# Second routed experts: inner units on the partitions, weights and biases loaded per block, no transposes between the products

## The chip, the cores and the metric

One core of one Trainium2 chip. The metric is the device time in microseconds (us) of one execution of the whole kernel, which is two transformer layers in one program. Five engines work side by side and meet at semaphores: TensorE (PE; its weight loads are listed as PEld), VectorE (DVE), ScalarE (ACT), GpSimd (POOL) and SyncE (SP, which here only issues DMAs).

## What is computed

`x` has 16 sequences of 256 rows of 128 numbers (4096 rows). Each layer is attention, layer norm, a mixture of experts, layer norm. The change is in the routed experts of the second layer:

```python
gates = xf @ router_w + router_b                      # 8 experts
topv, topi = jax.lax.top_k(gates, 2)
comb = einsum('nke,nk->ne', one_hot(topi, 8), softmax(topv))
h = gelu(einsum('nd,edh->enh', xf, w1) + b1[:, None, :])   # d = 128, h = 256
y = einsum('enh,ehd->end', h, w2) + b2[:, None, :]
moe_out = einsum('ne,end->nd', comb, y)
```

Two shared experts, which see every row, have the same form with weights `sw1`, `sw2` of their own. All data is float32.

## The kernel before

The program runs five stages one after the other, each with its own instruction stream per engine: `attention0`, `routed0` (first layer), `attention1`, `routed1` (second layer), `final1`.

`attention1` also routes: it scatters each normalised row twice, once for each of its two experts, into a table `xs` in memory, grouped by expert, with two more numbers behind the 128 of the row (where its result goes, and its first choice). In its last stretch, after the last sequence's attention, it computes the shared experts (`up`, `down`, `expert_hidden`, `expert_low`, 32 steps, L1589 on, L1768 on, L2202 on), the routing of the last two sequences, and on DVE a table of blocks (`table_counts` to `table_rows`): for each block of 256 rows its expert, the column of the expert's weights (`w_at`) and its first row in `xs` (`in_at`). Among these steps stand two pieces of set-up for `routed1`: the biases of the routed experts are fetched as rows on partitions 0 and 32 (SP, four small DMAs into `work`), `bias_high` rounds them and `bias_low` takes the rest (DVE, at steps 10, 11, 15 and 16), after a memset on POOL (L1932). Early in the stage SP loads the weights of all eight experts, 256 KB each, into `g.w` (L1268), where they stay.

`routed1` (L946 to L1090) goes over N = 39 blocks of 256 rows. For a block j:

- SP reads `in_at` into a register and loads the block's rows into one of 6 slots of `xrow` (L978 to L981); it waits for `dest_done`, that is for `destinations` of block j - 6.
- PE turns the rows (`turn_input`, two transposes, L1034), ACT copies the result to `x` (`turned`, L1057), two slots.
- `gate` (L1006, L1007): rows on the partitions, `x` is the stationary operand, the expert's 256 columns of `w1` stream by; a second product of ones with the bias rows adds the bias. ACT applies Gelu to 128x512 at once (L1052).
- `turn_hidden` (L1015): four transposes; DVE copies 128x512 from PSUM (`hidden_columns`, L1070).
- `down` (L1025, L1027): four products and two bias products; DVE copies 128x256 from PSUM to one of 4 slots of `yrow` (`output`, L1075).
- POOL scatters the 256 result rows to `yt` with two indirect DMAs (L989) to the rows in `dest`, which DVE computes (`destinations`, L1081).

The order on each engine is written out by hand. PE at step j: `gate(j)`, `turn_hidden(j - 1)`, `down(j - 2)`, `turn_input(j + 2)`. DVE at step j: `destinations(j)`, `hidden_columns(j - 1)`, `output(j - 2)`. `destinations(j)` overwrites the slot of block j - 4, so it first waits on `y_out`, which counts the landed scatters of block j - 4:

```python
dve.wait_ge(x_in[j % XSLOTS], (j // XSLOTS + 1) * 16)
after(dve, y_out[j % YSLOTS], j // YSLOTS * 32)
dve.wait_ge(xt_ps, j + 1)
```

DVE works in order, so `hidden_columns(j - 1)` and `output(j - 2)` stand behind this wait. `down(j)` waits for `y_done` of block j - 2 (two PSUM slots).

Of the kernel before, what the change touches and what calls it, by code (L numbers as in the profile page):

```python
# [12 lines left out]
F32 = mybir.dt.float32  # L13
# [8 lines left out]
P = 128  # L22
# [20 lines left out]
W1C = F1 + FB1 * P  # L43
LOW = 32
# [901 lines left out]
def routed1(nc, ctx, g, d):  # L946
# [3 lines left out]
    rc = lambda name: g.rc[:, RC[name][0]:sum(RC[name])]  # L950
    XSLOTS, YSLOTS = 6, 4
# [3 lines left out]
    xrow = sb("xrow", [P, XSLOTS, 2, XW])  # L955
    dest = sb("dest", [P, YSLOTS, 2], U32)
    x = sb("x", [P, 2, BR])
    hid, hid_t = sb("hid", [P, 2, 2, F1]), sb("hid_t", [P, 2, FB1, BR])
    yrow = sb("yrow", [P, YSLOTS, 2, P])
    G, HT, Y, XT = g.psum[:, 0:2, :], g.psum[:, 2:4, :], g.psum[:, 4:6, 0:BR], g.psum[:, 6:8, 0:BR]  # L960

    xt_ps, x_done, gate_ps, act_done, ht_ps, ht_done, down_ps, y_done, dest_done = (sem(n) for n in (
        "xt_ps", "x_done", "gate_ps", "act_done", "ht_ps", "ht_done", "down_ps", "y_done", "dest_done"))
    x_in = [sem(f"x_in{k}") for k in range(XSLOTS)]
    y_out = [sem(f"y_out{k}") for k in range(YSLOTS)]
# [7 lines left out]
    with nc.Block() as block:  # L973
        @block.sync
        def _(sp):
            for j in range(N):
                after(sp, dest_done, j - XSLOTS + 1)
                at = nc.values_load(in_at[0:1, j:j + 1], engines=(mybir.EngineType.SP,), min_val=0, max_val=XROWS - BR,  # L978
                                    skip_runtime_bounds_check_because="the table's rows are clamped")
                sp.dma_start(xrow[:, j % XSLOTS], g.xs[bass.ds(at, BR)].rearrange("(h p) f -> p h f", p=P)  # L980
                             ).then_inc(x_in[j % XSLOTS], 16)  # L981

# [12 lines left out]
        def _(pe):  # L995
            w = {}
            bias = g.q_stk[:, 0].rearrange("p h t -> p (h t)")

            def gate(j):
                w[j] = nc.values_load(w_at[0:1, j:j + 1], engines=(mybir.EngineType.PE,), min_val=0, max_val=(E1 - 1) * W1C,  # L1000
                                      skip_runtime_bounds_check_because="the table's rows are clamped")
                pe.wait_ge(x_done, j + 1)
                after(pe, act_done, j - 1)
                for h in range(2):
                    out = G[:, j % 2, h * F1:(h + 1) * F1]
                    nc.tensor.matmul(out, x[:, j % 2, h * P:(h + 1) * P], g.w[:, bass.ds(w[j], F1)], start=True, stop=False)  # L1006
                    last = nc.tensor.matmul(out, g.ones[:], bias[:, bass.ds(w[j] + P, F1)], start=False, stop=True)  # L1007
                last.then_inc(gate_ps, 1)

            def turn_hidden(j):  # L1010
                pe.wait_ge(act_done, j + 1)
                after(pe, ht_done, j - 1)
                for f in range(FB1):
                    for h in range(2):
                        last = nc.tensor.transpose(HT[:, j % 2, f * BR + h * P:f * BR + (h + 1) * P], hid[:, j % 2, h, f * P:(f + 1) * P],  # L1015
                                                   g.ident[:])
                last.then_inc(ht_ps, 1)

            def down(j):
                pe.wait_ge(ht_done, j + 1)  # L1020
                after(pe, y_done, j - 1)
                for h in range(2):
                    out = Y[:, j % 2, h * P:(h + 1) * P]
                    for f in range(FB1):
                        nc.tensor.matmul(out, hid_t[:, j % 2, f, h * P:(h + 1) * P], g.w[:, bass.ds(w[j] + (F1 + f * P), P)],  # L1025
                                         start=f == 0, stop=False)
# [1505 lines left out]
```

## Time and profile before

| | |
|---|---|
| median of 3 runs | 1634.45 us (1633.99 to 1639.09) |
| the profiled execution: its own time | 1633.04 us |
| its span in the profile | 1631.2 us |
| PE busy | 1392.3 us (85%) |
| DVE busy | 1077.9 us (66%) |
| ACT busy | 895.7 us (55%) |
| POOL busy | 647.9 us (40%) |
| `routed1`, first load issued to last scatter issued | 1436.8 to 1577.3 us |
| shared experts | 1378 to 1435 us |

Busy time counts an engine's instructions; matmuls are pipelined and their ends are modelled, so the time of one matmul in a row (its latency) is longer than the distance between two starts, and a PE busy for 90% of a stretch is not at 90% of its peak. Idle time is put down to what came last before the engine went on; "issue" there means that the profile shows nothing that it waited for, and records of DMA landings are incomplete in this trace.

### The profile page before, as it was taken

The page shows a single profiled execution, that of the slowest core. Times are in us where ns is not written, and L with a number is a line of the kernel's source. Part 1 is how long each engine was busy: PE and PEld are TensorE (multiplying, and loading weights), DVE is VectorE, ACT ScalarE, POOL GpSimd, SP SyncE. Part 2 cuts the span into 40 slices and gives each one's busy share as a digit, 9 for nine tenths or more (in the row PEclk, how much of TensorE's full clock was granted, in tenths as well). Part 3 has the DMA queues.
Part 4 walks back from the last instruction along what each step waited for, and adds up shares of the span by engine and source line. Part 5 has one row for each costly group of instructions (what it writes and reads, how often), then busy time and mean ns, then how long its engine had stood idle before and what let it go on. Part 6 is the DMA issues. An engine that isn't in the chain of part 4 may idle for free. (4 is left out here: it accounts for less than half of the span.)

```text
span 1631.2 us, 35670 instructions
## 1 busy us (share of the span) xinstructions
PE 1392.3 (85%) x10839; PEld 1132.1 (69%) x10840; DVE 1077.9 (66%) x3450; ACT 895.7 (55%) x2391; POOL 647.9 (40%) x978
## 2 busy tenths in 40 slices
PE   5999999999999998299998269999999998988840
PEld 4777777777777777188887157777777776778740
DVE  4777777777777776266665358888888874833326
ACT  3656666666666665055554136777666766832213
POOL 1344444444444444133333232344445333325542
PEclk9999999999999999599999559999999999999975
DMA  6112020202020200011111621022214000023214
GB/s 219 52 36 72 20 73 19 73 19 73 19 73 19 74 22 13 21 42 47 48 46 38 215 67 53 30 73 73 74 47 150 7 15 15 14 67 83 79 59 126
DMA packets 59992, 96.36 MB, mean 59 GB/s; under 512 B 11140, under 2 KB 49412, under 8 KB 57432
## 3 DMA queue, kind: packets, MB, share of 16 engines
q1 hardware_dynamic: 50632, 76.47, 15.3%
q0 software_dynamic: 8864, 18.43, 3.3%
q8 instruction: 34, 0.56, 0.1%
q10 hardware_dynamic: 432, 0.66, 0.1%
q14 instruction: 30, 0.25, 0.1%
HBM read 75.01 MB, written 61.60 MB: 84 GB/s over the span
## 5 line engine op out<-in xcount | busy, mean ns | idle before, releaser
L362 POOL TENSOR_TENSOR a_prob<-a_prob,a_rl 128x128 f32<-128x128 f32 (+1 forms) x258 | 125.5, 508 | 256.1 <-DVE a_rl L447 255.8
L250 ACT ACTIVATE a_prob<-psum,a_nmx 128x128 f32<-128x128 f32 (+1 forms) x516 | 212.3, 423 | 11.9 <-DVE a_nmx L442 11.9
L1989 DVE TENSOR_REDUCE a_mx<-psum 128x2 f32<-128x512 f32 x256 | 170.8, 689 | 41.8 <-PE psum L1320 38.1
L276 ACT ACTIVATE a_probt<-psum 128x768 f32<-128x768 f32 x128 | 103.9, 811 | 118.9 <-PE psum L639 118.9
L1680 ACT ACTIVATE a_prob<-psum 128x1024 f32<-128x1024 f32 x128 | 129.2, 1025 | 13.8 <-PE psum L1352 13.2
L441 DVE TENSOR_REDUCE a_nmx<-psum 128x2 f32<-128x256 f32 x130 | 55.2, 425 | 118.1 <-PE psum L592 118.1
L771 POOL DMA_INDIRECT yt<-m_yrow,m_dest x71 | 67.9, 956 | 158.6 <-DVE m_yrow L922 157.5
L639 PE MATMUL psum<-ident,a_prob 128*128 128x128 f32 x768 | 106.3, 275 | 14.0 <-DVE a_prob L451 14.0
L1320 PE MATMUL psum<-a_k_stk,q_stk 128*128 128x256 f32 x512 | 109.5, 312 | 3.1 <-DVE a_mx L1989 2.1
L288 ACT ACTIVATE a_ot<-psum,a_bias 128x256 f32<-128x256 f32 x128 | 61.4, 480 | 88.1 <-PE psum L665 84.2
L250 ACT ACTIVATION_READ_ACCUMULATOR a_prob<-psum,a_nmx 128x1 f32 x516 | 108.5, 210 | 0.0
L96 PE MATMUL psum<-a_xt_h,a_wqk_h 128*128 128x256 f32 x262 | 88.2, 337 | 23.2 <-DVE a_xt_l L426 16.3
L989 POOL DMA_INDIRECT yt<-m_yrow,m_dest x78 | 74.9, 960 | 79.3 <-DVE m_yrow L1075 56.6
L1349 PE MATMUL psum<-a_mt,a_pick 128*128 128x512 f32 x256 | 105.1, 410 | 0.0
L1352 PEld LDWEIGHTS psum<-q_stk,a_k_stk 128*128 128x128 f32 x512 | 96.4, 188 | 11.1
L1352 PE MATMUL psum<-q_stk,a_k_stk 128*128 128x256 f32 x512 | 102.0, 280 | 0.0
L1320 PEld LDWEIGHTS psum<-a_k_stk,q_stk 128*128 128x128 f32 x512 | 78.2, 195 | 31.7 <-issue 16.1
L639 PEld LDWEIGHTS psum<-ident,a_prob 128*128 128x128 f32 x768 | 86.3, 141 | 19.2 <-issue 16.4
L1674 ACT ACTIVATE q_stk<-psum,a_in_head 128x256 fp32r<-128x256 f32 x192 | 75.4, 476 | 31.2 <-PE psum L1314 29.2
L1871 POOL DMA_INDIRECT xs<-a_nrm,a_idx x64 | 65.8, 1027 | 58.4 <-DVE a_idx L2080 42.0
L442 DVE TENSOR_REDUCE a_nmx<-psum 128x2 f32<-128x512 f32 x130 | 88.5, 681 | 0.0
L356 POOL DMA_INDIRECT xs<-a_nrm,a_idx x64 | 64.8, 1012 | 52.3 <-issue 49.8
(346 smaller groups left out, 4245.4 us busy)
## 6 DMA issues: line engine op xcount, KB each, us to landing
xs<-in_fill SPq DMA_DIRECT2D x144, 264.0 KB
a_stage<-in_w SPq DMA_DIRECT2D x16, 384.0 KB, 4.3
m_xrow<-xs SPq DMA_DIRECT2D x39, 132.0 KB
m_xrow<-xs SPq DMA_DIRECT2D x71, 66.0 KB, 1.8
a_yin<-yt SPq DMA_DIRECT2D x16, 256.0 KB, 2.8
f_yin<-yt SPq DMA_DIRECT2D x8, 512.0 KB, 4.1
yt<-m_yrow,m_dest POOLq DMA_INDIRECT x149, 2.2
a_xin<-in_x SPq DMA_DIRECT2D x17, 128.0 KB, 2.1
```

The lines of the kernel that those rows point to most:

```text
L96: nc.tensor.matmul(out, wh, xh, start=start, stop=False)
L250: last = nc.scalar.activation(prob[:, slot, h, at], S[:, 2 * slot + h, at], ACT.Exp, bias=nmx[:, slot, q, h:h + 1], accum_out=lsum[:, slot ...
L276: nc.scalar.activation(probt[:, hp % 2], PT[:, :, 0:SW], ACT.Copy).then_inc(pt_done, 1)
L362: last = nc.gpsimd.tensor_tensor(prob[:, slot, 0, at], prob[:, slot, 0, at], rl[:, slot, 0, q:q + 1].to_broadcast(prob[:, slot, 0, at].sha ...
L442: nc.vector.reduce_max(nmx[:, slot, 1, :], S[:, 2 * slot:2 * slot + 2, P:SW], AX.X, negate=True).then_inc(nmx_done, 1)
L639: last = nc.tensor.transpose(PT[:, h, t * P:(t + 1) * P], prob[:, hp % 2, h, t * P:(t + 1) * P], g.ident[:])
L1320: last = nc.tensor.matmul(bank[:, q * T:(q + 1) * T], q_stk[:, p, h, q * P:(q + 1) * P], k_stk[:, p, h // HG, :], start=True, stop=True)
L1349: nc.tensor.matmul(out.rearrange("p (k q) -> p k q", k=QB), pick[:, h:h + 1].to_broadcast([P, P]), mt[:, p].unsqueeze(1).to_broadcast([P, ...
L1352: last = nc.tensor.matmul(out[:, k * T:(k + 1) * T], k_stk[:, p, h // HG, k * P:(k + 1) * P], q_stk[:, p, h, :], start=False, stop=k == QB ...
L1674: nc.scalar.activation(q_stk[:, p, k * HG + j, :], bank[:, 0:T], ACT.Identity, scale=in_head[:, j:j + 1])
L1680: nc.scalar.activation(prob[:, k % 2, 2 * (t % 2):2 * (t % 2) + 2, :], ST[:, 2 * (t % 2):2 * (t % 2) + 2, :], ACT.Exp, scale=SCALE).then_i ...
L1989: nc.vector.reduce_max(mx[:, :, h:h + 1], bank.rearrange("p (q k) -> p q k", q=QB), AX.X).then_inc(mx_done, 1)
```

## The change

In `routed1` the first product has the inner units on the partitions: the expert's weights are the stationary operand and the turned rows `x` stream by (256 columns). Its result is already what the second product needs as stationary operand, so `turn_hidden`, `hidden_columns` and their two slots go. The bias of the units is one number per partition and goes into ACT's Gelu, now two instructions of 128x256; the bias of the output is a row that stands on all partitions and is added by DVE where it copied. The four bias products go. PE at step j: `up(j)`, `down(j - 1)`, `turn_input(j + 2)`; DVE: `destinations(j)`, `output(j - 1)`.

The expert's weights and both biases (642 numbers per partition, 321 KB) are loaded for every block by SP into one of 4 slots `w`, in front of the load of the rows of block j + 2; a slot comes free with `y_done` of the block four before. In `attention1` the loads of `g.w` (8 of 256 KB), the four small loads, the memset on POOL, `bias_high` and `bias_low` go. `w_at` counts in units of 642.

```diff
+W1R = W1C + FB1 + P
-    XSLOTS, YSLOTS = 6, 4
+    XSLOTS, WSLOTS, YSLOTS = 6, 4, 4
...
-            for j in range(N):
-                after(sp, dest_done, j - XSLOTS + 1)
...
+            def rows(j):
+                after(sp, dest_done, j - XSLOTS + 1)
+                sp.dma_start(xrow[:, j % XSLOTS], g.xs[bass.ds(at(in_at, j, XROWS - BR), BR)]...).then_inc(x_in[j % XSLOTS], 16)
+            def weights(j):
+                after(sp, y_done, j - WSLOTS + 1)
+                sp.dma_start(w[:, j % WSLOTS, :], d["wr1"][:, bass.ds(at(w_at, j, (E1 - 1) * W1R), W1R)]
+                             ).then_inc(w_in[j % WSLOTS], 16)
+            for j in range(-2, N):
+                if 0 <= j:
+                    weights(j)
+                if j + 2 < N:
+                    rows(j + 2)
...
+            def up(j):
                 pe.wait_ge(x_done, j + 1)
                 after(pe, act_done, j - 1)
-                for h in range(2):
-                    nc.tensor.matmul(out, x[:, j % 2, h * P:(h + 1) * P], g.w[:, bass.ds(w[j], F1)], start=True, stop=False)
-                    last = nc.tensor.matmul(out, g.ones[:], bias[:, bass.ds(w[j] + P, F1)], start=False, stop=True)
+                pe.wait_ge(w_in[j % WSLOTS], (j // WSLOTS + 1) * 16)
+                for f in range(FB1):
+                    last = nc.tensor.matmul(H[:, j % 2, f * BR:(f + 1) * BR], w[:, j % WSLOTS, f * P:(f + 1) * P], x[:, j % 2, :],
+                                            start=True, stop=True)
...
-            def turn_hidden(j):
...
+            def down(j):
                 pe.wait_ge(act_done, j + 1)
                 after(pe, y_done, j - 1)
                 for h in range(2):
                     for f in range(FB1):
+                        last = nc.tensor.matmul(Y[:, j % 2, h * P:(h + 1) * P], hid[:, j % 2, f, h * P:(h + 1) * P],
+                                                w[:, j % WSLOTS, F1 + f * P:F1 + (f + 1) * P], start=f == 0, stop=f == FB1 - 1)
-                    last = nc.tensor.matmul(out, g.ones[:], bias[:, bass.ds(w[j], P)], start=False, stop=True)
...
+                for f in range(FB1):
+                    last = nc.scalar.activation(hid[:, j % 2, f, :], H[:, j % 2, f * BR:(f + 1) * BR], ACT.Gelu,
+                                                bias=w[:, j % WSLOTS, W1C + f:W1C + f + 1])
...
-            def hidden_columns(j):
...
-                nc.vector.tensor_copy(yrow[:, j % YSLOTS]..., Y[:, j % 2, :]).then_inc(y_done, 1)
+                nc.vector.tensor_tensor(yrow[:, j % YSLOTS], Y[:, j % 2, :]...,
+                                        w[:, j % WSLOTS, W1C + FB1:W1R].unsqueeze(1).to_broadcast([P, 2, P]), ALU.add
+                                        ).then_inc(y_done, 1)
...
-            for e in range(E1):
-                sp.dma_start(g.w[:, e * W1C:(e + 1) * W1C], d["w1"][:, e * W1C:(e + 1) * W1C]).then_inc(w_in, 16)
```

The order of DVE's instructions for three blocks in `routed1`, before (`m_dest` is `destinations`, `m_hid_t` is `hidden_columns`, `m_yrow` is `output`):

```order
L1081 SCALAR_TENSOR_TENSOR m_dest<-m_xrow,expert 128x2
L1070 COPY m_hid_t<-psum 128x512
L1075 COPY m_yrow<-psum 128x256
L1081 SCALAR_TENSOR_TENSOR m_dest<-m_xrow,expert 128x2
L1070 COPY m_hid_t<-psum 128x512
L1075 COPY m_yrow<-psum 128x256
```

and now:

```order
L1078 SCALAR_TENSOR_TENSOR m_dest<-m_xrow,expert 128x2
L1070 TENSOR_TENSOR m_yrow<-psum,m_w 128x256
L1078 SCALAR_TENSOR_TENSOR m_dest<-m_xrow,expert 128x2
L1070 TENSOR_TENSOR m_yrow<-psum,m_w 128x256
L1078 SCALAR_TENSOR_TENSOR m_dest<-m_xrow,expert 128x2
L1070 TENSOR_TENSOR m_yrow<-psum,m_w 128x256
```

The wide copy is gone, and the output behind `destinations(j)` is that of block j - 1, not j - 2.

SP's queue in the middle of `routed1`, before (a register is read, then the rows of a block are loaded):

```order
L978 TENSOR_LOAD in_at
L980 ISA
L980 DMA m_xrow<-xs 128x2x132
L978 TENSOR_LOAD in_at
L980 ISA
L980 DMA m_xrow<-xs 128x2x132
```

and now:

```order
L979 TENSOR_LOAD w_at
L989 REGISTER_ALU
L989 DMA m_w<-in_wr 128x642
L979 TENSOR_LOAD in_at
L984 ISA
L984 DMA m_xrow<-xs 128x2x132
```

Each block has two register reads and two DMAs where it had one of each, and the rows stand behind the weights.

## Rows read from the trace of the kernel before

**Rows 1.** Stretches; columns: engines' busy us (instructions), granted clock, DMA share, GB/s.

```profile
1437.00:1441.00 4.00, 1.59 (x5) 1.03 (x6) 0.32 (x2) 0.56 (x2) 0.00 (x0) 0.50 0.51 117
...
1449.00:1577.40 128.40, 110.20 (x807) 102.01 (x805) 44.17 (x110) 33.38 (x70) 74.90 (x78) 0.98 0.26 72
...
1530.00:1550.00 20.00, 16.20 (x122) 14.98 (x121) 6.81 (x18) 5.29 (x11) 10.83 (x12) 1.00 0.30 81
...
1569.00:1573.00 4.00, 3.94 (x20) 3.94 (x20) 1.28 (x3) 0.00 (x0) 2.35 (x3) 0.57 0.09 32
```

**Rows 2.** Timeline of POOL: the scatters; columns: start, us, engine, line, tiles, [idle before].

```profile
1449.01 0.96 POOL L989 DMA_INDIRECT yt<-m_yrow,m_dest  x1 [25.85 <-DVE m_yrow L1075]
...
1453.10 0.96 POOL L989 DMA_INDIRECT yt<-m_yrow,m_dest  x1 [0.30 <-issue]
1456.02 0.96 POOL L989 DMA_INDIRECT yt<-m_yrow,m_dest  x1 [1.96 <-DVE m_yrow L1075]
...
1575.11 0.96 POOL L989 DMA_INDIRECT yt<-m_yrow,m_dest  x1 [0.30 <-issue]
1576.37 0.96 POOL L989 DMA_INDIRECT yt<-m_yrow,m_dest  x1 [0.31 <-issue]
```

**Rows 3.** Waits of DVE from 1449 to 1577.4: us in total, times, longest.

```profile
DVE m_dest L1081 <- issue: 40.3, 19, 4.0
DVE m_dest L1081 <- DMA yt<-m_yrow,m_dest: 16.7, 9, 3.2
```

**Rows 4.** Timeline of DVE in the same stage.

```profile
1454.81 0.42 DVE L1075 COPY m_yrow<-psum 128x256 f32<-128x256 f32 x1 [1.40 <-PE psum L1027]
1457.20 0.28 DVE L1081 SCALAR_TENSOR_TENSOR m_dest<-m_xrow,expert 128x2 uint32<-128x2 f32 x1 [1.97 <-DMA yt<-m_yrow,m_dest]
```

**Rows 5.** Timeline of PE: one step of `routed1` without a wait, and the next step's start.

```profile
1447.57 0.41 PE L1034 MATMUL psum<-ident,m_xrow 128*128 128x128 f32 x2
1447.81 0.60 PE L1006 MATMUL psum<-w,m_x 128*128 x2
...
1448.91 0.60 PE L1015 MATMUL psum<-ident,m_hid 128*128 128x128 f32 x4
1449.35 0.61 PE L1025 MATMUL psum<-w,m_hid_t 128*128 x4
...
1450.41 0.41 PE L1034 MATMUL psum<-ident,m_xrow 128*128 128x128 f32 x2
```

**Rows 6.** Timeline of SP and PE at the start of `routed1`.

```profile
1436.82 3.00 SPq L980 DMA_DIRECT2D m_xrow<-xs  x4
...
1439.10 0.69 PE L1034 MATMUL psum<-ident,m_xrow 128*128 128x128 f32 x2 [4.94 <-DMA m_xrow<-xs]
...
1440.58 1.19 PE L1006 MATMUL psum<-w,m_x 128*128 x2
```

**Rows 7.** Groups by line from 1449 to 1577.4: ACT's copy of 128x256.

```profile
L1057 ACT ACTIVATE m_x<-psum 128x256 f32<-128x256 f32 x34 | 13.1, 385 | 52.2 <-PE psum L1034 31.1 <-DMA a_sb<-in_m_sb 18.1 <-issue 2.8
```

**Rows 8.** DMA: queues from 1449 to 1577.4 (MB, share); whole run: KB each, us to landing.

```profile
q1 hardware_dynamic: 8160, 4.06, 13.9%
q0 software_dynamic: 2464, 5.05, 11.3%
...
a_yin<-yt SPq DMA_DIRECT2D x16, 256.0 KB, 2.8
f_yin<-yt SPq DMA_DIRECT2D x8, 512.0 KB, 4.1
```

**Rows 9.** A stretch at the start of `attention1`, the engines' columns as in rows 1.

```profile
915.00:925.00 10.00, 2.31 (x8) 1.65 (x8) 2.85 (x10) 0.88 (x3) 7.13 (x9) 0.50 0.98 335
```

**Rows 10.** Shared experts, 1376 to 1435: PE's wait for DVE; the bias work on DVE.

```profile
PE psum L96 <- DVE q_stk L2205: 2.7, 6, 0.8
...
L2218 DVE CAST q_stk<-a_work 1x1536 fp32r<-1x1536 f32 x4 | 4.0, 1006 | 0.0
L2223 DVE TENSOR_TENSOR q_stk<-a_work,q_stk 1x1536 fp32r<-1x1536 f32 x2 | 3.5, 1749 | 0.1
```

More of the change, by code:

```diff
@@ L975, in _, with at @@
         def _(sp):
[L976 removed]
+            def at(table, j, most):
+                return nc.values_load(table[0:1, j:j + 1], engines=(mybir.EngineType.SP,), min_val=0, max_val=most,
+                                      skip_runtime_bounds_check_because="the table's rows are clamped")
+            def rows(j):
                 after(sp, dest_done, j - XSLOTS + 1)
[L978 to L980 removed]
+                sp.dma_start(xrow[:, j % XSLOTS], g.xs[bass.ds(at(in_at, j, XROWS - BR), BR)].rearrange("(h p) f -> p h f", p=P)
                              ).then_inc(x_in[j % XSLOTS], 16)
+            def weights(j):
[7 more added lines that the diff above has]
+                    rows(j + 2)
         @block.gpsimd
@@ L1010, in turn_hidden @@
-            def turn_hidden(j):
-                pe.wait_ge(act_done, j + 1)
[L1012 to L1020, printed above, removed]
+                pe.wait_ge(w_in[j % WSLOTS], (j // WSLOTS + 1) * 16)
@@ L1035, in turn_input @@
                 last.then_inc(xt_ps, 1)
-            for j in range(-2, N + 2):
+            for j in range(-2, N + 1):
                 if 0 <= j < N:
-                    gate(j)
-                if 0 <= j - 1 < N:
-                    turn_hidden(j - 1)
-                if 0 <= j - 2:
-                    down(j - 2)
+                    up(j)
+                if 0 <= j - 1:
+                    down(j - 1)
                 if j + 2 < N:
@@ L1060, in _ @@
                 if 0 <= j:
-                    gate(j)
+                    units(j)
                 if j + 2 < N:
@@ L1082, in destinations @@
                                                xrow[:, j % XSLOTS, :, P], ALU.not_equal, ALU.add).then_inc(dest_done, 1)
-            for j in range(N + 2):
+            for j in range(N + 1):
                 if j < N:
                     destinations(j)
-                if 0 <= j - 1 < N:
-                    hidden_columns(j - 1)
-                if 0 <= j - 2:
-                    output(j - 2)
+                if 0 <= j - 1:
+                    output(j - 1)
 def attention1(nc, ctx, g, d):
@@ L1154, in attention1 @@
     nrm = sb("nrm", [P, 2, QB, XW])
-    work = sb("work", [P, E1 // 2 * (P + F1)])
-    stage = work[:, 0:S1 * W1C]
+    stage = sb("stage", [P, S1 * W1C])
     th, pr = sb("th", [P, NTL]), sb("pr", [P, NTL, 2])
@@ L1179, in attention1 @@
     hid_h, hid_l = (flat(q_stk[:, 1])[:, a * W * GT:(a + 1) * W * GT].rearrange("p (d n) -> p d n", n=GT) for a in range(2))
-    EH = E1 // 2
-    rows32 = work[:].rearrange("p (e n) -> p e n", e=EH)
-    brows = flat(q_stk[:, 0]).rearrange("p (e n) -> p e n", e=E1)
     TB = NB1 + 1
```

90 lines of the change are left out of this document (28 added, 62 removed).

## Prediction

> **What bounds the kernel now.** I read the stretches first, then POOL's timeline, DVE's waits, and PE's steps. The change touches two places: the routed experts of the second layer, 1436.8 to 1577.3 us, and the shared experts before them.
>
> In the routed stage PE looks like the bound: busy 110.2 of 128.4 us, at 0.98 of the clock [rows 1]. It isn't, all the time. A step of PE without a wait takes 1450.41 - 1447.57 = 2.84 us [rows 5]. But from the first scatter (1449.01) to the last (1576.37) are 127.36 us [rows 2], that is 38 blocks at (127.36 - 1.27) / 38 = 3.32 us. The missing 0.48 us a block stands in DVE's waits: 40.3 + 16.7 = 57.0 us in front of `m_dest` [rows 3], part of it mere slack. This is `destinations(j)`, which waits until the scatters of block j - 4 have landed. The round trip, read once: the second scatter of a block is issued at 1453.10 [rows 2]; the `m_dest` that waits for this block starts at 1457.20 [rows 4], 4.1 us later. Behind `m_dest` DVE has the copy of hidden columns and only then `output(j - 2)`. So block j - 2 can't be scattered before block j - 4 has landed: **two blocks to a round trip**. From the end of an output copy (1454.81 + 0.42) to its first scatter (1456.02) pass another 0.8 us [rows 2, 4]. The trip is then 1.27 (first scatter to second) + 2.3 to 4.1 (landing; the low end is that of a load of rows, 1439.10 - 1436.82 [rows 6]) + 0.7 (`m_dest`, wide copy) + 0.42 + 0.8 = 5.5 to 7.3 us, or 2.7 to 3.6 us a block; 3.32 lies inside.
>
> POOL's own floor: two scatters follow each other at 1576.37 - 1575.11 = 1.26 us [rows 2], so a block can't take less than 2.53 us.
>
> **The change, part by part.**
>
> *PE in the routed stage.* Of the 2.84 us, the four transposes go (1449.35 - 1448.91 = 0.44) [rows 5]. Of `gate` (1448.91 - 1447.81 = 1.10) and `down` (1450.41 - 1449.35 = 1.06) [rows 5] the bias products go. A bias product has the same columns as a weight product, in one pass where float32 is two instructions; I take a fifth of 1.10 and an eighth of 1.06, 0.35 in all. PE's step becomes about 2.05 us, and 2.4 if the bias products were free before. Both lie under POOL's 2.53, so this choice moves no number. PE's register read goes too, under the same cover.
>
> *ACT and DVE.* ACT has two Gelus of 256 columns and one copy of 256, at 385 ns each [rows 7]: 1.2 us a block. DVE has `m_dest`, 0.22 to 0.28, and one add of 256 columns, for which I take the copy's 0.42 [rows 4]: 0.7 us. Neither bounds.
>
> *The round trip.* The output behind `destinations(j)` is now that of block j - 1, so block j - 1 needs the landing of block j - 4: **three blocks to a trip**. The trip loses the wide copy: 1.27 + 2.3 to 4.1 + 0.25 + 0.42 + 0.8 = 5.0 to 6.8 us, 1.7 to 2.3 us a block, below POOL's 2.53. This is the main effect of the change, more than PE's shorter step.
>
> *The new loads.* Each block adds a load of 321 KB. SP: four loads are issued in 3.00 us, about 0.88 us each with the register read [rows 6]; two to a block are 1.8 of 2.53 us, so SP holds. Landing: 2.8 us for 256 KB, 4.1 us for 512 KB [rows 8]; by the line between them 3.1 us. A slot comes free with `y_done(j - 4)`, and `down(j - 1)` stands behind `up(j)` on PE, so this trip also has three blocks: 0.5 (register read and wake-up) + 3.1 + about 0.9 (`up`) + 0.9 (`down`) + 0.5 (add) + 0.3 (semaphores, an estimate) = 6.2 us against 3 x 2.53 = 7.6. Bounds of the landing: 2.8, and 10 us if the queue were as full as at the start of `attention1` (share 0.98) [rows 9]. I take 3.1, since the queue will not be full: rows and scatters keep the 16 DMA engines busy for (13.9 + 11.3)% of 128.4 / 39 = 0.83 us a block [rows 8], and 321 KB (0.329 MB) at 335 GB/s / 0.98 [rows 9] add 0.96. That is 1.8 of 2.53 us, 71%.
>
> A rule of the Trainium skill speaks against this change: by "DMA: Bandwidth & Descriptors", section "Issuing engines are not separate DMA queues", loads from SP and scatters from POOL run on the same 16 DMA engines and interleave. The share of 0.30 in today's stage [rows 1] cannot show what 0.71 does to the landings; what it could do is the first rival.
>
> *Sum for the stage.* POOL bounds, with some blocks held up by a late landing: I take 2.60 us a block (floor 2.53; the trips leave 0.8 to 2.6 and 1.4 us, and a scatter as late as the one of 4.1 us that fuller queues hold up by 1 us more would use that up). First to last scatter: 38 x 2.60 + 1.26 = 100.1 us, against 127.4: **-27.3 us**.
>
> *Start of the stage.* Now from the first issue at 1436.82 [rows 6] to the first scatter 12.2 us. The first weights are issued third, 1.8 us after the first rows, and land 3.1 us later, at +4.9; today the first product starts at +3.8 [rows 6]. Against this 1.1 us, a whole pipeline step (transposes, wide copy, second wait) goes from the fill, but the second weights are issued only at +3.5 and PE runs at 0.50 of its clock there [rows 1]. I take -0.6; bounds +2 and -2.5.
>
> *Shared experts.* The bias work takes 4.0 + 3.5 = 7.5 us of DVE [rows 10], and a memset of POOL. PE waits for DVE's low halves for 2.7 us in all [rows 10], mostly beside this work. I take -2.0; bounds 0 and -4.
>
> *Start of `attention1`.* 2.1 MB of loads go from a full queue (share 0.98 [rows 9]). Nothing that waits there needs what stands behind them: 0, within 1 us. The cover is the long chain of small steps of the first sequence.
>
> **Sum:** -27.3 - 0.6 - 2.0 = -29.9. Profiled execution 1633.0 - 29.9 = 1603.1 us. The median of the runs is 1.4 us above the profiled one: **1604.5 us**. 0.3% of this kernel is 5 us, about what a measurement can tell from no change.
>
> **Rivals.**
>
> 1. *The DMA engines bound.* Loads and scatters delay each other, and both trips grow. With 2.5 us more, the weights' trip is 8.7 us, 2.9 us a block: 38 x 2.9 + 1.26 = 111.5, -15.9 - 2.6 = -18.5, **1616 us**. For: the share of 0.71, and loads in a row at 0.98 [rows 9]. Against: 0.7 us a block is left. Chance 0.15.
>
> 2. *Slower: PE's clock falls.* PE now has idle time in every block (2.05 of 2.60 us used). Where PE paused after 1566, the clock came back at 0.57 (1569 to 1573) [rows 1], the lower level of 1.2 GHz for most of it. At that level a step takes 2 x 2.05 = 4.1 us: 38 x 4.1 + 1.26 = 157.1, +29.7 - 2.6, **1661 us**. It decides when the mean passes (127.4 + 2.6 - 1.3) / 38 = 3.39 us, that is when more than half of the blocks run at the low level. Against: from 1530 to 1550 PE was busy 16.2 of 20 us and kept 1.00 [rows 1]; the new share, 2.05 us and the tails of the products, is about the same. Chance 0.05. "TensorE: Matmul & The Clock Gate", in the section "Why this matters for your kernels" of the Trainium skill, warns of the same: idle gaps between bursts of matmuls send the clock back to its lower level. The pause before 1569 agrees; the stretch from 1530 says that gaps as short as these don't.
>
> 3. *The trip doesn't shorten.* If weights or rows tie the blocks so that 3.32 us stay, only the start and the shared experts are left: -2.6, **1632 us**, no measurable change. The weights' landing would have to be 3 x 3.32 - 3.1 = 6.9 us. Chance 0.05.
>
> **How the numbers follow.** Forecast 0.75. Its own range: 2.53 us a block with both small gains at their bounds, 97.4 + start -2.5 + shared -4: 1598; 2.75 us with none: 1613. The first rival reaches to 1616, and a little more of it to 1618. Range 1597 to 1618. Faster 0.90 (forecast and first rival), same 0.05 (third), slower 0.05 (second).
>
> **What would show it.** Scatters of POOL in an even beat of 1.27 us with hardly a pause, some 99 to 101 us from first to last. DVE's waits in front of `m_dest` on landed scatters become short. PE's clock at 1.00 and its waits spread over all steps. SP's loads of weights land within 4 us and PE's `up` seldom waits for them. In the shared experts PE's waits for `q_stk` below 1 us. The forecast is wrong if the beat breaks: if PE waits for `m_w` (rival 1), or the clock is at its lower level in the stage (rival 2), or `m_dest` still waits as long as now (rival 3).

## The result, and the profile after

| | kernel before | changed kernel |
|---|---|---|
| median | 1634.30 us (1631.11 to 1642.68, 9 runs) | 1626.02 us (1622.15 to 1629.19, 9 runs) |
| ratio, 95% interval | | 0.9945 (0.9927 to 0.9962) |
| profiled execution, span | 1633.04, 1631.2 us | 1629.15, 1627.3 us |

The change gives 8 us where 30 were forecast, and 1626 us lies outside the range of 1597 to 1618. The sign was right. On some other chips both kernels are faster: on chip 0 the changed one takes 1594.7 us beside 1613.8 us for the kernel before. That is told at the end of the experiments.

The span by parts, from the starts of the same instructions in both profiles:

| part | before | after | difference | forecast |
|---|---|---|---|---|
| up to the first work of the shared experts | 1378.73 | 1382.29 | +3.6 | 0, within 1 |
| shared experts, first to last `expert_low` on DVE (L2205, now L2183) | 52.27 | 49.70 | -2.6 | -2.0 |
| from there to the first load of `routed1` | 5.82 | 5.58 | -0.2 | |
| first load to first scatter | 12.19 | 12.04 | -0.2 | -0.6 |
| first to last scatter | 127.36 | 122.91 | -4.5 | -27.3 |
| last scatter to the end | 54.83 | 54.79 | 0.0 | |

One term is wrong by far: the steady blocks, (122.91 - 1.27) / 38 = 3.20 us each instead of 2.60. The stage in the profile after, a piece of its start and all from the first scatter to the last, with the columns of [rows 1]:

```profile
1438.00:1442.00 4.00, 1.38 (x4) 0.58 (x4) 0.44 (x2) 0.77 (x2) 0.00 (x0) 0.50 0.65 167
1449.60:1573.80 124.20, 86.76 (x517) 74.48 (x515) 21.79 (x74) 42.40 (x109) 74.68 (x78) 0.92 0.59 170
```

The instructions shrank as forecast: PE 110.2 to 86.8 us, DVE 44.2 to 21.8 us, and the DMA share rose from 0.26 [rows 1] to 0.59. But no engine is full any more: POOL works 74.7 of 124.2 us. POOL's timeline shows how it misses its floor (start, duration, engine, line, operation; idle time before it and what ended it in brackets):

```profile
1494.61 0.97 POOL L1004 DMA_INDIRECT yt<-m_yrow,m_dest  x1 [0.30 <-issue]
...
1499.67 0.96 POOL L1004 DMA_INDIRECT yt<-m_yrow,m_dest  x1 [0.31 <-issue]
1500.94 0.96 POOL L1004 DMA_INDIRECT yt<-m_yrow,m_dest  x1 [0.30 <-issue]
1504.86 0.95 POOL L1004 DMA_INDIRECT yt<-m_yrow,m_dest  x1 [2.97 <-DVE m_yrow L1070]
```

The beat of 1.26 us is there, as in [rows 2], mostly for three or four blocks; then comes a pause of 2 to 3 us. From 1492.09 us on, the blocks start 2.52, 2.54, 2.53 and 5.19 us apart. In the pause POOL waits for DVE. What DVE, ACT and PE do in it:

```profile
1500.13 0.22 DVE L1078 SCALAR_TENSOR_TENSOR m_dest<-m_xrow,expert 128x2 uint32<-128x2 f32 x1 [1.84 <-DMA yt<-m_yrow,m_dest]
1503.65 0.42 DVE L1070 TENSOR_TENSOR m_yrow<-psum,m_w 128x256 f32<-128x256 f32 x1 [3.30 <-DMA a_prob<-in_sel]
```

```profile
1499.29 0.38 ACT L1057 ACTIVATE m_x<-psum 128x256 f32<-128x256 f32 x1 [2.47 <-DMA a_sb<-in_m_sb]
1503.55 0.84 ACT L1050 ACTIVATE m_hid<-psum,m_w 128x256 f32<-128x256 f32 x2 [3.88 <-remote]
```

```profile
1497.48 1.10 PE L1016 MATMUL psum<-m_x,m_w 128*128 128x256 f32 x4 [0.43 <-issue]
1498.42 1.05 PE L1025 MATMUL psum<-m_w,m_hid 128*128 128x128 f32 x8
...
1504.45 1.16 PE L1025 MATMUL psum<-m_w,m_hid 128*128 128x128 f32 x8 [3.59 <-ACT m_hid L1050]
1505.44 0.38 PE L1033 MATMUL psum<-ident,m_xrow 128*128 128x128 f32 x2
1505.66 1.64 PE L1016 MATMUL psum<-m_x,m_w 128*128 128x256 f32 x4
```

Read them together. The names of the releasers (`a_prob`, `a_sb`, "remote") can't be right: none of these is in this stage. By the program the Gelu of line 1050 waits for PE's product of line 1016, which by its row ended at 1498.58, and starts at 1503.55, 5.0 us later. The addition of line 1070 waits for line 1025, ended at 1499.47, and starts 4.2 us later. Elsewhere in the stage both start 0.04 us after the product's end. The semaphore records say the same: those of PE's signals for the products that ended at 1498.58, 1499.47, 1499.69 and 1500.86 stand at 1503.53, 1503.62, 1503.66 and 1503.72. The four products start 0.4 to 0.9 us apart (1497.48, 1498.42, 1499.31 and 1499.73), the four signals come 0.04 to 0.09 us apart: it is not the products that are late. **PE's signals are held back and come in a burst.** (Whether it is the signal itself that is held, or the end of the write that it reports, no record tells.) In the window from the first to the last addition, 50 of the 98 recorded signals of PE come over 0.3 us after the modelled end of the last product (longest 4.2 us). In the kernel before it is 61 of 129 (longest 2.7 us), so late signals were there already. (The delays are lower bounds: they start at the last product ended, and some signals have no record.) Not all late signals come in bursts: between the bursts single ones get through, up to 2.5 us late, while POOL scatters. And only PE's are late: from 1449 to 1560 us it is 47 of 91 recorded signals of PE, but none of 47 of ACT, 47 of DVE and 24 of POOL.

The waits in the stage (us in total, times, longest):

```profile
POOL yt L1004 <- DVE m_yrow L1070: 52.8, 14, 25.5
DVE m_yrow L1070 <- PE psum L1025: 42.3, 21, 4.9
ACT m_hid L1050 <- PE psum L1016: 25.2, 20, 2.5
DVE m_dest L1078 <- DMA yt<-m_yrow,m_dest: 24.1, 10, 3.9
...
PE psum L1016 <- DMA m_w<-in_wr: 6.6, 5, 1.4
```

PE waits for weights in only five blocks, so the new loads are not what holds the stage. The shared experts went as forecast; PE's wait for `q_stk` fell from 2.7 us [rows 10] to this:

```profile
PE psum L97 <- DVE q_stk L2183: 0.7, 1, 0.7
```

### The profile page after: what moved, and what is told of

Its sections match the earlier page's. It is cut to its first block and busy times, and to the rows that moved or that the text cites. A ratio compares the mean times of both kernels' runs of the same rounds, so it can differ in the third digit from the quotient of the medians.

```text
span 1627.3 us, 34872 instructions
## 1 busy us (share of the span) xinstructions
PE 1367.8 (84%) x10527; PEld 1104.3 (68%) x10528; DVE 1046.5 (64%) x3405; ACT 903.0 (55%) x2430; POOL 642.4 (39%) x977
## 5 line engine op out<-in xcount | busy, mean ns | idle before, releaser
L1661 ACT ACTIVATE a_prob<-psum 128x1024 f32<-128x1024 f32 x128 | 129.2, 1025 | 13.0 <-PE psum L1333 12.5
L1301 PE MATMUL psum<-a_k_stk,q_stk 128*128 128x256 f32 x512 | 110.2, 315 | 2.8 <-DVE a_mx L1967 2.1
L1004 POOL DMA_INDIRECT yt<-m_yrow,m_dest x78 | 74.7, 957 | 74.7 <-DVE m_yrow L1070 52.8
L640 PEld LDWEIGHTS psum<-ident,a_prob 128*128 128x128 f32 x768 | 86.4, 141 | 19.1 <-issue 16.4
```

Of the source, the lines that this page charges most:

```text
L640: last = nc.tensor.transpose(PT[:, h, t * P:(t + 1) * P], prob[:, hp % 2, h, t * P:(t + 1) * P], g.ident[:])
L1301: last = nc.tensor.matmul(bank[:, q * T:(q + 1) * T], q_stk[:, p, h, q * P:(q + 1) * P], k_stk[:, p, h // HG, :], start=True, stop=True)
L1661: nc.scalar.activation(prob[:, k % 2, 2 * (t % 2):2 * (t % 2) + 2, :], ST[:, 2 * (t % 2):2 * (t % 2) + 2, :], ACT.Exp, scale=SCALE).then_i ...
```

## The experiments

Each run is compared with runs of the kernel before on the same chip. "Late" is the count as above, and "block" the mean distance of two blocks' first scatters (for e6_no_scatter that of its additions on DVE). The chips are those that the results name; for the first result none is named.

| run | chip | before, us | this, us | ratio (95%) | block, us | late |
|---|---|---|---|---|---|---|
| e1_first_four | 7 | 1634.94 | 1623.02 | 0.9938 (0.9912 to 0.9964) | 3.14 | 57 of 97 |
| e2_before_loads | 7 | 1634.94 | 1640.56 | 1.0048 (1.0020 to 1.0076) | 3.52 | 63 of 125 |
| e3_more_slots | 7 | 1634.94 | 1624.21 | 0.9941 (0.9920 to 0.9962) | 3.17 | 56 of 97 |
| e4_double_loads | 7 | 1634.94 | 1627.73 | 0.9953 (0.9932 to 0.9975) | 3.26 | 45 of 90 |
| e5_one_scatter | 9 | 1635.18 | 1582.47 | 0.9680 (0.9646 to 0.9714) | 2.22 | 0 of 60 |
| e6_no_scatter | 9 | 1635.18 | 1581.99 | 0.9658 (0.9626 to 0.9690) | 2.23 | 5 of 111 |
| e7_less_pe | 9 | 1635.18 | 1621.62 | 0.9917 (0.9885 to 0.9949) | 3.16 | 44 of 86 |
| e8_before_one_scatter | 9 | 1635.18 | 1609.16 | 0.9831 (0.9805 to 0.9856) | 2.77 | 0 of 144 |
| e9_half_width | 13 | 1617.23 | 1594.87 | 0.9859 (0.9804 to 0.9913) | 2.53 | 0 of 107 |
| e10_half_rows | 13 | 1617.23 | 1588.84 | 0.9816 (0.9763 to 0.9868) | 2.42 | 0 of 105 |
| e11_apart | 13 | 1617.23 | 1591.14 | 0.9828 (0.9771 to 0.9885) | 2.57 | 0 of 113 |
| e12_paced | 13 | 1617.23 | 1594.07 | 0.9850 (0.9796 to 0.9904) | 2.54 | 0 of 109 |
| e13_after_again | 9 | 1630.17 | 1619.64 | 0.9941 (0.9917 to 0.9964) | 3.11 | 49 of 96 |
| e14_apart_again | 9 | 1630.17 | 1626.04 | 0.9968 (0.9945 to 0.9990) | 3.46 | 48 of 91 |
| e15_paced_more | 1 | 1614.88 | 1619.72 | 1.0026 (1.0006 to 1.0046) | 3.15 | 0 of 111 |
| e16_half_width_again | 1 | 1614.88 | 1594.40 | 0.9878 (0.9850 to 0.9906) | 2.53 | 0 of 109 |
| e17_half_rows_again | 1 | 1614.88 | 1589.16 | 0.9839 (0.9815 to 0.9862) | 2.41 | 0 of 106 |
| e18_after_third | 0 | 1613.78 | 1594.70 | 0.9880 (0.9856 to 0.9905) | 2.53 | 0 of 107 |

**Is it the loads, or the slots? (chip 7)**

e1_first_four loads weights only for the first four blocks:

```diff
-                if 0 <= j:
+                if 0 <= j < WSLOTS:
                     weights(j)
...
-                pe.wait_ge(w_in[j % WSLOTS], (j // WSLOTS + 1) * 16)
+                pe.wait_ge(w_in[j % WSLOTS], 16)
```

> The changed kernel, but the weights are loaded for the first four blocks only and stay in the four slots (later blocks use another expert's weights, so the routed part of the second layer is computed with wrong weights). All instructions of the other engines are the same; 35 loads of 321 KB go. In the changed kernel a block takes 3.20 us from first to last scatter (122.9 us), in beats of 2.53 us with a pause of 2 to 2.7 us every third to fifth block, in which ACT and DVE start up to 4 us after the end of the product they wait for. Theory A (the loads' traffic makes those signals and landings late): the pauses go, 2.53 to 2.65 us a block, 98 to 102 us, total 1626 - 22 = 1604 us. Theory B (too few slots for the time a landing takes): the trip of the weights is gone too, so also about 2.6 us. Theory C (the late signals belong to PE and the order of the stage, not to the loads): 3.1 to 3.2 us a block, total within 4 us of 1626.

e2_before_loads is the kernel before with an unused load of 321 KB behind each load of rows:

```diff
+                sp.dma_start(spare[:, j % 4, :], d["wr1"][:, j % E1 * 642:(j % E1 + 1) * 642]).then_inc(extra[j % 4], 16)
```

> The kernel before, with a load of 321 KB per block added behind each load of rows, into four slots that nobody reads. Theory A (traffic makes signals late): a block goes from 3.32 to 3.6 us or more, total 1634 + 10 to 25 us. Theory B (slots): the added loads tie nothing, so only the scatters' landings could be later: 0 to +5 us. Theory C (not the loads): 1634 within 3 us.

e3_more_slots:

```diff
-    XSLOTS, WSLOTS, YSLOTS = 6, 4, 4
+    XSLOTS, WSLOTS, YSLOTS = 8, 6, 8
```

> The changed kernel with 8 slots for rows, 6 for weights and 8 for results in place of 6, 4 and 4. Theory A: late signals from PE hit just the same; a little is absorbed: 3.0 to 3.2 us a block, total 1620 to 1626. Theory B: 2.53 to 2.7 us a block, total 1603 to 1610. Theory C: as A.

e4_double_loads puts that unused load behind every load of weights of the changed kernel.

> The changed kernel with a second load of 321 KB per block into four slots that nobody reads. Engines' share of DMA would be 0.7 + 0.3 of the time: near 1.0 at 3.2 us a block. Theory A: clearly slower, 3.8 us a block or more, total 1626 + 23 or more. Theory B: the weights' own landing gets later by the load in front of it, 1 us or more, so the trip of three blocks grows by 0.3 us a block and more: 1626 + 12 or more. Theory C: only if the DMA engines are full does it get slower: within 8 us of 1626.

With the loads gone, the stage's DMA share falls to 0.27 and the pauses stay:

```profile
1448.00:1567.00 119.00, 84.80 (x492) 73.18 (x490) 20.39 (x71) 40.72 (x104) 71.91 (x76) 0.88 0.27 77
```

A block still takes 3.14 us, with more slots 3.17, with twice the loads 3.26. Two profiles of the unaltered changed kernel stand 0.09 us apart (3.20, and 3.11 in e13_after_again), so 0.06 us for the traffic or 0.03 for the slots can't be told from nothing; the 0.6 us of the pauses they are not. In the kernel before the same load costs 0.2 us a block in the profile and 5.6 us in the median. The first rival of the prediction, the DMA engines as the bound, falls, and with it the landings as what breaks the beat. Late signals appear in all four.

**Is it PE, or POOL's scatters? (chip 9)**

e5_one_scatter stores only the first half of each block, with the waits on landings halved (e8_before_one_scatter is the same edit in the kernel before):

```diff
-                for h in range(2):
+                for h in range(1):
                     nc.gpsimd.indirect_dma_start(g.yt, ...
```

> The changed kernel with one scatter per block in place of two in this stage (the second half of every block's rows is not stored; the buffer they go to is filled with 4 MB of zeros at the end of the attention stage instead, whose price is some us there). If the pauses come from POOL's two scatters standing back to back (theory D), they go, and a block takes what PE needs, 1.97 to 2.1 us, so the stage is about 42 us shorter. If they are PE's own (theory E), PE's signals are still held back every few blocks for 2 to 5 us, and a block takes 1.97 us plus the same 0.67 us of pauses, about 2.6 us.

> The kernel before with one scatter per block in place of two (half of the rows are not stored; the same 4 MB of zeros). PE's step there was 2.84 us by the trace. Theory D: a block falls from 3.32 to 2.84 us, no signal is late. Theory E: late signals stay and a block takes 3.2 us or more.

e6_no_scatter stores four blocks and no more:

```diff
-                for h in range(2):
+                for h in range(2 if j < YSLOTS else 0):
```

> The changed kernel in which only the first four blocks are scattered (the rows of the other 35 are not stored; the buffer is filled with zeros as in the kernel above). Theory D: no pause after the fourth block, 2.0 us a block. Theory E: pauses go on to the end at the same distance in blocks. That holds for any theory in which the traffic of the scatters or their semaphores delay PE: only with pauses in this run is PE alone their source.

e7_less_pe computes half of the second product:

```diff
-                    for f in range(FB1):
-                        last = nc.tensor.matmul(Y[...], ..., start=f == 0, stop=f == FB1 - 1)
+                    for f in range(1):
+                        last = nc.tensor.matmul(Y[...], ..., start=True, stop=True)
```

> The changed kernel with half of PE's second product in this stage (only the first 128 of 256 hidden units are summed, so PE works 0.45 us less a block, 1.52 instead of 1.97 us; everything else stays). Theory E, held signals in proportion to PE's work: pauses come every 5 blocks rather than 4, and the mean block falls from 3.20 to about 3.05 us. Theory D: POOL's beat is as before, 3.20 us a block.

With one scatter a block no signal is late in this stage in either kernel. POOL in e8_before_one_scatter goes evenly at PE's step of 2.84 us [rows 5] until the last few blocks:

```profile
1480.56 0.96 POOL L989 DMA_INDIRECT yt<-m_yrow,m_dest  x1 [1.89 <-DVE m_yrow L1075]
1483.41 0.96 POOL L989 DMA_INDIRECT yt<-m_yrow,m_dest  x1 [1.89 <-DVE m_yrow L1075]
1486.25 0.96 POOL L989 DMA_INDIRECT yt<-m_yrow,m_dest  x1 [1.89 <-DVE m_yrow L1075]
```

The changed kernel with one scatter goes at 2.22 us a block, 0.25 above PE's step without a wait. e7_less_pe, on the same chip, has 44 late signals and 3.16 us a block though PE works 0.45 us a block less (by its expectation 3.05 us if PE's work set the rate, 3.20 if not; with two unaltered profiles at 3.20 and 3.11 this run alone wouldn't decide). e6_no_scatter shows the onset. Six scatters go in the beat, then a pause, then the last two. One signal is 1.4 us late while the six still go (at 1449.28), the other four late ones come in the pause (1452.87 to 1453.76), and behind the last two scatters none is late. The scatters around the pause, and the addition that comes late there:

```profile
1450.03 0.96 POOL L1004 DMA_INDIRECT yt<-m_yrow,m_dest  x1 [0.30 <-issue]
1451.30 0.96 POOL L1004 DMA_INDIRECT yt<-m_yrow,m_dest  x1 [0.30 <-issue]
1454.89 0.96 POOL L1004 DMA_INDIRECT yt<-m_yrow,m_dest  x1 [2.63 <-DVE m_yrow L1070]
```

```profile
1447.84 0.43 DVE L1070 TENSOR_TENSOR m_yrow<-psum,m_w 128x256 f32<-128x256 f32 x1 [1.56 <-PE psum L1025]
...
1453.68 0.42 DVE L1070 TENSOR_TENSOR m_yrow<-psum,m_w 128x256 f32<-128x256 f32 x1 [3.32 <-DMA a_prob<-in_sel]
```

Theory D, the scatters hold PE's signals, stands; theory E, that PE holds them by itself, falls by e5, e6 and e8.

**What of the scatters? (chip 13, where the question vanished)**

e9_half_width stores 64 of 128 values of each row, e10_half_rows 64 of 128 rows:

```diff
-  g.yt, bass.IndirectOffsetOnAxis(ap=dest[:, j % YSLOTS, h:h + 1], axis=0), yrow[:, j % YSLOTS, h, :]
+  g.yt.rearrange("r (a f) -> (r a) f", a=2), ...ap=dest[:, j % YSLOTS, h:h + 1]..., yrow[:, j % YSLOTS, h, 0:P // 2]
or
+  g.yt, ...ap=dest[0:P // 2, j % YSLOTS, h:h + 1]..., yrow[0:P // 2, j % YSLOTS, h, :]
```

> The changed kernel whose 78 scatters store 64 of a row's 128 values (rows of 256 instead of 512 bytes, to other places of the zeroed buffer; half of the result is not stored). The instruction on POOL takes the same 0.96 us with 128 rows. If the bytes that the scatters write set the pace (theory G), late signals go and a block takes POOL's 2.53 us. If the rows or the instructions set it (theory H), a block stays at 3.1 us with the pauses.

> The changed kernel whose 78 scatters store only partitions 0 to 63, so 64 rows of 512 bytes each (half of the result is not stored). As many bytes as in the kernel above, as many instructions as in the changed one, half the rows. If the number of rows sets the pace (theory H1), late signals go. If the number of scatters does (theory H2), a block stays at 3.1 us. The instruction itself may get shorter, then a block could fall to PE's 2.0 to 2.2 us.

e11_apart adds the output bias to the incoming rows and not to the second product, so its result isn't the experts', and POOL need not wait for PE:

```diff
             def output(j):
-                dve.wait_ge(down_ps, j + 1)
+                dve.wait_ge(w_in[j % WSLOTS], (j // WSLOTS + 1) * 16)
...
-                nc.vector.tensor_tensor(yrow[:, j % YSLOTS], Y[:, j % 2, :].rearrange("p (h n) -> p h n", h=2),
+                nc.vector.tensor_tensor(yrow[:, j % YSLOTS], xrow[:, j % XSLOTS, :, 0:P],
```

(SP then waits for PE's `xt_ps` and `down_ps` too before it fills a slot again, and PE no longer for `y_done`.)

> The changed kernel in which the addition on DVE takes the block's incoming rows instead of the second product and does not wait for it (the output is not the experts'), so that POOL's chain no longer hangs on PE, and PE's no longer on the addition; only the weight and row slots hold POOL at most 4 blocks ahead of PE. Theory D says that the scatters hold PE's signals back: POOL then keeps its beat of 2.53 us through the time in which PE's signals are late, PE's signals are still late, longer than now if they come free only when POOL rests. If instead POOL itself has a rate below its beat (a theory that PE's signals are late for some other reason and POOL only waits), the beat breaks although POOL waits for nothing of PE.

e12_paced keeps the full result and puts a small memset behind each scatter:

```diff
                                                  yrow[:, j % YSLOTS, h, :], None).then_inc(y_out[j % YSLOTS], 16)
+                    nc.gpsimd.memset(pad[:, 2 * j + h, :], 0.0)
```

> The changed kernel with a small memset on POOL behind each scatter, some 0.15 us, so that POOL's beat is about 2.8 us a block instead of 2.53. If only scatters standing directly back to back hold PE's signals (theory D1), a steady 2.8 us a block follows, 12 us faster than the changed kernel. If there is a mean rate of about 1.55 us per scatter above which a backlog grows (theory D2), the first late signal comes later than now, but the mean stays at 3.1 us a block.

All four came out without a late signal, and the kernel before beside them at 1617 us instead of 1634. e12_paced gives it away: its memset fits into the 0.3 us that POOL leaves between two scatters anyway, so it is in effect the changed kernel, with a beat of 1.27 us. The expectation of "about 2.8 us" for its beat was wrong:

```profile
1480.35 0.96 POOL L1005 DMA_INDIRECT yt<-m_yrow,m_dest  x1 [0.17 <-issue]
1481.32 0.14 POOL L1007 MEMSET m_pad<- 128x32 f32 x1
1481.62 0.96 POOL L1005 DMA_INDIRECT yt<-m_yrow,m_dest  x1 [0.17 <-issue]
```

So these runs couldn't tell bytes from rows from spacing. They raised another question: is it the chip? The traces at hand already say something on it. `attention1` scatters too, in groups of four 1.3 us apart (`xs`), and no edit touches these scatters. Between 1000 and 1360 us, 38 to 48 of some 620 recorded signals of PE are late in both first profiles and in every run on chips 7 and 9, all within 2.3 us of the start of a scatter; in every run on chips 13, 1 and 0 it is none of some 635. e5_one_scatter has 48 late there and none in `routed1`. So chip 13 shows none whatever the edit, and the first result was taken on a chip like 7 and 9.

**The chip, and who waits for whom (chips 9, 1 and 0)**

> The changed kernel as it is, a second time. The last four runs were taken beside runs of the kernel before of 1617 us, all others beside 1634 to 1635 us, and none of the last four has a late signal of PE although one of them is the changed kernel with its beat of 2.54 us. So the late signals may belong to the chip that a job gets (theory K), not to the edits of those four runs. Theory K: beside a kernel before of 1617 us this one takes about 1594 us with a block of 2.4 to 2.54 us and no late signal; beside one of 1634 us it takes 1626 us with the late signals as in its first profile. If late signals show beside 1617 us, or none beside 1634 us, theory K falls.

> The kernel in which POOL's chain does not hang on PE, again. On a chip with late signals (before near 1634 us): if the scatters hold the signals back (theory D), POOL keeps 2.53 us a block through the time in which PE's signals are late, and PE's signals are late at least as often as in the changed kernel. On a chip without them (before near 1617 us) it repeats its run: 1591 us, none late.

The unaltered changed kernel on chip 9: 49 of 96 signals late, 3.11 us a block, ratio 0.9941, near the 0.9945 of the first result. e14_apart_again is the run that shows the direction. POOL hangs on PE here only through slots that are four blocks deep. Its scatters, then ACT's and PE's rows of the same time:

```profile
1466.50 0.95 POOL L1006 DMA_INDIRECT yt<-m_yrow,m_dest  x1 [0.30 <-issue]
1467.76 0.96 POOL L1006 DMA_INDIRECT yt<-m_yrow,m_dest  x1 [0.30 <-issue]
...
1475.33 0.96 POOL L1006 DMA_INDIRECT yt<-m_yrow,m_dest  x1 [0.31 <-issue]
1476.60 0.96 POOL L1006 DMA_INDIRECT yt<-m_yrow,m_dest  x1 [0.30 <-issue]
```

```profile
1472.37 0.38 ACT L1058 ACTIVATE m_x<-psum 128x256 f32<-128x256 f32 x1 [4.10 <-DMA a_sb<-in_m_sb]
1477.32 0.84 ACT L1051 ACTIVATE m_hid<-psum,m_w 128x256 f32<-128x256 f32 x2 [4.57 <-remote]
1479.52 0.38 ACT L1058 ACTIVATE m_x<-psum 128x256 f32<-128x256 f32 x1 [1.36 <-DMA a_sb<-in_m_sb]
```

```profile
1468.37 1.10 PE L1018 MATMUL psum<-m_x,m_w 128*128 128x256 f32 x4
1469.31 1.05 PE L1026 MATMUL psum<-m_w,m_hid 128*128 128x128 f32 x8
...
1478.21 2.08 PE L1026 MATMUL psum<-m_w,m_hid 128*128 128x128 f32 x8 [4.28 <-ACT m_hid L1051]
```

PE's product that ended at 1469.47 is answered by ACT only at 1477.32, 7.8 us later, and in all that time POOL scatters every 1.26 us. That signal still gets through alone, at 1477.30; the burst, three signals up to 9.1 us late, comes at 1479.5, behind POOL's last scatter (1476.60 + 0.96 = 1477.56), when its slots have run out. The holds are longer than in e13_after_again, with POOL tied to PE (longest 9.1 us against 4.3), and a block takes 3.46 us. In the changed kernel POOL starves sooner, rests sooner, and PE is freed sooner: 1503.53 is 1.6 us behind the end of the scatter of 1500.94.

e15_paced_more has a memset of 400 columns, with its own semaphore:

```diff
+                    after(pool, padded, 2 * j + h)
+                    nc.gpsimd.memset(pad[:], 0.0).then_inc(padded, 1)
```

> The changed kernel with a memset of 128x400 values on POOL behind each scatter, about 0.45 us of which 0.3 us fit between two scatters, so a beat of 2.8 to 2.9 us a block. On a chip with late signals (before near 1630 us): only back-to-back scatters hold signals (D1): 2.85 us a block, about 10 us faster than the changed kernel; a mean rate above which a backlog grows (D2): first late signal later, mean still 3.05 to 3.2 us. On a chip without them (before near 1617 us): 2.85 us a block, 12 us slower than the changed kernel would be.

> The kernel whose scatters store rows of 256 bytes, again. On a chip with late signals: if bytes set them off (theory G) none is late and a block takes 2.53 us; if rows or instructions do (theory H) a block takes 3.1 us. On a chip without them it repeats 1595 us.

> The kernel whose scatters store 64 rows, again. On a chip with late signals: 2.42 us a block and none late if the rows or the bytes set them off, 3.1 us if the number of scatter instructions does. On a chip without them it repeats 1589 us.

These fell on chip 1, again without a late signal. The memset took 0.45 us and the beat became 3.15 us a block, not 2.85: 0.17 us pass behind the memset, too, so only 0.13 of the 0.30 us between two scatters take it in:

```profile
1481.35 0.96 POOL L1007 DMA_INDIRECT yt<-m_yrow,m_dest  x1 [0.17 <-issue]
1482.31 0.45 POOL L1010 MEMSET m_pad<- 128x400 f32 x1
1482.93 0.97 POOL L1007 DMA_INDIRECT yt<-m_yrow,m_dest  x1 [0.17 <-issue]
```

It still says something: 0.62 us a block more on POOL cost 38 x 0.62 = 23.6 us, against 25 us between its time and that of the changed kernel on such a chip (1619.7 and 1594.7). There POOL's scatters are the bound, one for one.

> The changed kernel as it is, a third time. On a chip whose kernel before takes 1615 to 1617 us: no late signal, a beat of 2.53 us a block, about 1594 us, a ratio near 0.986. On one whose kernel before takes 1630 to 1635 us: late signals, 3.1 us a block, a ratio near 0.994. A mixture of the two (late signals at 1615 us, or none at 1632 us) would speak against the chip as what decides it.

The changed kernel on chip 0, from the first scatter on, and POOL's first and last scatters:

```profile
1438.90:1536.00 97.10, 81.17 (x519) 69.90 (x517) 21.20 (x74) 44.53 (x109) 73.71 (x77) 1.00 0.77 217
```

```profile
1439.11 0.96 POOL L1004 DMA_INDIRECT yt<-m_yrow,m_dest  x1 [24.39 <-DVE m_yrow L1070]
1440.37 0.96 POOL L1004 DMA_INDIRECT yt<-m_yrow,m_dest  x1 [0.30 <-DVE m_yrow L1070]
...
1535.08 0.96 POOL L1004 DMA_INDIRECT yt<-m_yrow,m_dest  x1 [0.30 <-issue]
1536.34 0.96 POOL L1004 DMA_INDIRECT yt<-m_yrow,m_dest  x1 [0.30 <-issue]
```

(1536.34 - 1439.11 - 1.26) / 38 = 2.53 us a block, PE's clock at 1.00, DMA share 0.77. The waits in front of `m_dest` are long, and cost nothing, since POOL never stops:

```profile
DVE m_dest L1078 <- DMA yt<-m_yrow,m_dest: 62.8, 33, 2.8
...
PE psum L1016 <- DMA m_w<-in_wr: 7.3, 17, 0.9
```

So the same program has two outcomes. Chips 7 and 9 (kernel before at 1630 to 1635 us): late signals in every run, in `routed1` in every one that scatters twice a block, ratio 0.994 (chip 9; on chip 7 the unaltered changed kernel was not run). Chips 0, 1 and 13 (kernel before at 1614 to 1617 us): none in any run, ratio 0.988 for the changed kernel. No chip showed both at two full scatters a block. No version with the full result was found that is clearly faster than the changed kernel; by the intervals that one is faster than the kernel before on both kinds, by 0.6% and 1.2%. The gain of 30 us was reached on neither: on chip 0 it is 19.1 us.

**What stays open.** What of a scatter holds the signals (its bytes, rows or number): the runs meant for it met chips without holds. Whether spacing helps on chips 7 and 9: not tried there. By what path POOL's scatters reach PE's signals, why PE's alone, and why only on some chips: no record shows it. Only chip 9 was met twice, with the same outcome both times; that it is the chip, and not something else that came with it, rests on that. `routed0` adds one thing on spacing: its scatters stand 2.8 us apart (first profile after), and none of some 335 signals of PE is late there in any run. And every time here belongs to an execution with a profile's records, so whether signals are late without them can't be said.

## Why the prediction was wrong, point by point

- **"Sum for the stage. POOL bounds ... I take 2.60 us a block."** This step failed. It measured 3.20 us, -4.5 instead of -27.3 us. POOL's floor of 2.53 us is real (chips 0, 1, 13 hold it for 97 us), but on the chip of the result scatters at the floor hold PE's signals, and the pause gives the gain back: of the distances between bursts of three signals or more six are 12.7 to 13.0 us, with four blocks between, and three are 9.9 to 10.1, with three, as if one beat of 2.53 were left out each time. The forecast took the floor from two neighbouring scatters in [rows 2]; that such a pair can be kept up for a whole stage was assumed.
- **"Two blocks to a round trip"** as the cause of 3.32 us before. The reading was at best half right. The 57 us in front of `m_dest` [rows 3] were taken as a trip that bounds; e18_after_third has 62.8 us of the same wait and loses nothing by it. In [rows 3], 40.3 us were marked "issue", a wait for which the profile has no releaser, up to 4.0 us long, and the prediction put them to the same cause without asking what else was late there. 61 of 129 signals of PE were. With one scatter the kernel before goes at PE's 2.84 us, but that edit also shortens the trip by 1.27 us, so it doesn't separate the two. The kernel before is 13 to 21 us faster on chips without late signals, which suggests that part of the 3.32 us belonged to the chip; it isn't shown, since its block was not profiled there. It would also be why the forecast of -30 isn't met on chip 0, where the block does take 2.53 us: the forecast set POOL's floor against a block of 3.32 us that itself held late signals.
- **PE's step** of 2.05 us: right. Between 1450.14 and 1452.11, with no wait, it took 1.97 us.
- **ACT and DVE**: right in effect. The Gelu takes 0.47 us rather than 0.385, the addition 0.42.
- **The new loads**: SP holds, and PE waits for weights 6.6 us in five blocks. Share forecast 71%, measured 0.59 at 3.20 us a block and 0.77 at 2.53. Leaving out all but four of the loads gains no more than 0.06 us a block. The warning of the Trainium skill, "DMA: Bandwidth & Descriptors", section "Issuing engines are not separate DMA queues", that loads and scatters share the same 16 DMA engines, cost little here: one more load a block added 0.06 us in e4_double_loads, and 0.2 us in the kernel before (e2_before_loads).
- **Start of the stage**: -0.2 against -0.6. **Shared experts**: -2.6 against -2.0. **Ahead of them**: +3.6 where 0 was forecast; 1.2 of it stands before any edited instruction, so it is the difference of two executions, and the rest grows within `attention1`. Its late signals don't explain that, with 43 before and 45 after; the cause is open.
- **Rivals.** The first (DMA engines, 1616 us) named a time nearer to the result for a wrong reason. The second, PE's clock, came as a consequence only: 0.92 in the stage, with the product of line 1016 at 1.64 instead of 1.10 us behind a pause; on chip 0 PE is busy 81.2 of 97.1 us and keeps 1.00. The third (3.32 us stay) came nearest in size, 1632 us, also for another reason. None of the three had the mechanism.

## What to carry to other kernels

A floor read from two neighbouring instructions is a floor for two; before a stage is costed at it, look for a stretch in which the engine already runs at it, and if there is none, widen the range. When an engine starts late, compare its start with the end of the instruction that the program makes it wait for, not with the releaser's name in a row: that difference is 0.04 us as a rule and up to 5 us in the pauses. It was in the trace of the kernel before, with signals up to 2.7 us late, and would have told of the held signals. And where a result may hang on the chip, run the unaltered kernel beside the edits, look for a stretch that no edit touches and that shows the same effect, and keep the time of the kernel before next to every verdict.

## What the runs showed of the hardware

- On chips 7 and 9 PE's semaphore signals are held back while POOL issues indirect scatters of 128 rows of 512 bytes every 1.26 us: by the count up to 6.3 us late with POOL waiting for PE (e3_more_slots), up to 9.1 us where it does not. The signals of ACT, DVE and POOL itself are not. On chip 9, at one scatter in 2.2 or 2.85 us, no signal of PE was late. Single late signals come while POOL scatters; bursts of three or more came 0.9 to 1.7 us behind the end of the last scatter in the first profile after, and 1.9 us behind it in the pause of e14_apart_again.
- On chips 0, 1 and 13 none was late at the same beat, nor in `attention1`, and the kernel before took 1614 to 1617 us instead of 1630 to 1635.
- A scatter costs POOL 0.96 us and 0.30 us behind it; a memset of 0.14 us fits into that gap at no cost (1.27 us apart, e12_paced), one of 0.45 us lengthens the distance of two scatters from 1.26 to 1.58 us. Half as wide rows change nothing (2.53 us a block), half the rows little (2.42 us).
